# A windowed attention stage with sinks: ScalarE's and VectorE's pieces of a round in another order

## The reference, cut to what matters

```python
q = (x @ Wq.T + bq).reshape(B, S, 64, 64).transpose(0, 2, 1, 3)
k = (x @ Wk.T + bk).reshape(B, S, 8, 64).transpose(0, 2, 1, 3)    # each serves 8 query heads
v = (x @ Wv.T + bv).reshape(B, S, 8, 64).transpose(0, 2, 1, 3)
scores = jnp.einsum('bhqd,bhkd->bhqk', q, k) * scale
allowed = (qi >= kj) & (qi - kj < WINDOW)
scores = jnp.where(allowed[None, None], scores, -1e30)
logits = jnp.concatenate([scores, sink], axis=-1)
probs = jax.nn.softmax(logits, axis=-1)[..., :-1]
o = jnp.einsum('bhqk,bhkd->bhqd', probs, v)
return o.transpose(0, 2, 1, 3).reshape(B, S, H * HD) @ Wo.T + bo
```

## Time and profile before

| | us |
|---|---|
| median of 3 runs | 3887.63 (3885.69 to 3892.8) |
| the profiled execution | 3892.8 |
| its span in the profile | 3891.0 |
| PE busy | 3547.9 (91%) |
| DVE busy | 3078.6 (79%) |
| ACT busy | 2233.3 (57%) |
| POOL busy | 1442.3 (37%) |

### The profile page before, as it was taken

How to read it: one execution, slowest core, us unless ns; L and a number is a source line. 1 busy time by engine, 2 the same in 40 slices (tenths; PEclk the granted TensorE clock), 3 DMA queues, 4 the chain that set the end, 5 groups by cost and what they waited for, 6 DMA issues and landing times.

```text
span 3891.0 us, 93870 instructions
## 1 busy us (share of the span) xinstructions
PE 3547.9 (91%) x32894; PEld 2474.4 (64%) x32894; DVE 3078.6 (79%) x11272; ACT 2233.3 (57%) x6991; POOL 1442.3 (37%) x1741
## 2 busy tenths in 40 slices
PE   7999999999999989999989969989878999899955
PEld 5888888888888866666644433335556666555532
DVE  6989999999999966677779967767876778788771
ACT  5888888888888852257654433433333222467611
POOL 2455455455445510045448855520010000222117
PEclk8999999999999989889999989999988999799958
DMA  3000000000000012210000000000000000000023
GB/s 129 3 3 3 3 3 3 3 3 3 3 3 3 3 44 92 72 66 2 2 1 1 0 11 0 1 1 1 1 1 34 1 1 1 33 2 2 23 60 49
DMA packets 30897, 64.58 MB, mean 17 GB/s; under 512 B 3424, under 2 KB 19808, under 8 KB 29152
## 3 DMA queue, kind: packets, MB, share of 16 engines
q1 hardware_dynamic: 24288, 52.29, 3.8%
q0 software_dynamic: 6144, 6.30, 1.0%
HBM read 49.93 MB, written 8.65 MB: 15 GB/s over the span
## 4 chain that ended last, share of the span: by engine, by line
PE 67%; DVE 19%; issue 5%; ACT 5%; POOL 2%; DMA 1%; DVEq 0%; POOLq 0%; ACTq 0%; SPq 0%
PE ps L176 8%; PE ps L537 7%; PE ps L497 7%; PE ps L521 6%; PE ps L473 5%; PE ps L1674 3%; PE ps L1645 3%; PE ps L1643 3%; PE ps L2285 3%; PE ps L2298 3%; DVE gbbc L2337 2%; PE ps L1014 2%; DVE gbbc L2326 2%; DVE gbbc L2332 2%; PE ps L992 2%
## 5 line engine op out<-in xcount | busy, mean ns | idle before, releaser
L736 ACT ACTIVATE T<-T 128x128 f32<-128x128 f32 x1024 | 397.0, 398 | 11.6 <-DVE T L663 11.6
L736 ACT ACTIVATE W<-T 128x128 f32<-128x128 f32 x1024 | 396.9, 398 | 3.7 <-DVE T L663 3.7
L643 DVE CUSTOM_DVE_ANT_0 T<-ps,C 128x128 f32<-128x128 f32 x1536 | 381.3, 286 | 0.0
L653 DVE COPY_PREDICATED W<-gbbc,ps 128x512 f32<-128x512 int32 x512 | 342.5, 722 | 3.0 <-PE ps L176 2.5
L497 PE MATMUL ps<-T 64*64 64x192 f32 (+2 forms) x8192 | 317.8, 292 | 16.9 <-DVE T L643 16.9
L537 PE MATMUL ps<-W,gbbc 64*64 64x128 f32 (+1 forms) x6912 | 319.7, 310 | 2.0 <-DVE W L653 1.2
L497 PEld LDWEIGHTS ps<-T 64*64 64x64 f32 x8192 | 256.4, 133 | 95.8 <-issue 60.9
L176 PE MATMUL ps<-C,T 128*128 128x128 f32 (+1 forms) x1620 | 263.9, 301 | 50.4 <-DVE T L307 18.9
L1241 POOL TENSOR_TENSOR QK<-T,QK 128x512 fp32r<-128x512 f32 x128 | 162.0, 1275 | 383.3 <-ACT T L1201 264.9
L537 PEld LDWEIGHTS ps<-W,gbbc 64*64 64x64 f32 x6912 | 280.0, 132 | 28.2 <-PE ps L537 23.0
L827 POOL TENSOR_TENSOR W<-W,T 128x512 f32<-128x512 f32 x256 | 260.8, 1040 | 77.5 <-DVE T L670 77.5
(11 more groups left out here) (420 smaller groups left out, 8826.8 us busy)
## 6 DMA issues: line engine op xcount, KB each, us to landing
T<-crow_dram SPq DMA_DIRECT2D x128, 128.0 KB, 3.0
W<-in_l1f_dram SPq DMA_DIRECT2D x1, 6152.0 KB, 18.0
W<-in_l0a_dram SPq DMA_DIRECT2D x1, 5172.5 KB, 25.4
W<-in_l2f_dram SPq DMA_DIRECT2D x1, 3160.0 KB, 10.6
W<-in_l3f_dram SPq DMA_DIRECT2D x1, 3076.0 KB, 9.9
W<-in_sm_dram SPq DMA_DIRECT2D x1, 2729.0 KB, 9.0
W<-in_l0f_dram SPq DMA_DIRECT2D x1, 2256.0 KB, 30.2
X<-in_x_dram SPq DMA_DIRECT2D x1, 2048.0 KB, 7.4
```

Source lines behind the costliest of these rows:

```text
L643: done(e.tensor_tensor_reduce(sm[:, at:at + 128], src, m, 1.0, -3.0e38, ALU.add, ALU.max, mx[:, col:col + 1]), s["masked"], x == (3 if ban ...
L653: e.copy_predicated(a.PT[t % 2][:, 512 + 512 * j:1024 + 512 * j].rearrange("p (h w) -> p h w", h=4), is_.unsqueeze(1).broadcast_to([P, 4, ...
L736: done(e.activation(a.Pr[i % 4][:, at:at + w_], a.Sm[i % 2][:, at:at + w_], ACT.Exp, bias=a.ngs[i % 4][:, c:c + 1], scale=a.scale, accum_o ...
```

## The change

Two loops are written in another order. No instruction is added, taken away or altered.

On ACT, a full round's pieces between `outputs(2 * leaving)` and `sinks(2 * n)` are ordered anew: three of the weights of unit 2n come before the second `outputs`, three behind it, then `turned(2 * turning)`, and only then `project(ahead)`; the last two weights follow. On DVE, `parted(2 * turning)` and `shift(2 * n + 1)` change places.

```diff
@@ attention_dve
         if n is not None:
             masks(2 * n + 1)
+        if turning is not None:
+            parted(2 * turning)
         if n is not None:
             shift(2 * n + 1)
-        if turning is not None:
-            parted(2 * turning)
         if kv is not None:
             project(*kv)
@@ attention_act
         if leaving is not None:
             outputs(2 * leaving)
+        if n is not None:
+            begin(2 * n)
+            weights(2 * n, 0, 3)
+        if leaving is not None:
             outputs(2 * leaving + 1)
         if n is not None:
-            begin(2 * n)
-            weights(2 * n, 0, 4)
+            weights(2 * n, 3, 6)
+        if turning is not None:
+            turned(2 * turning)
         if ahead is not None:
             project(ahead)
-        if turning is not None:
-            turned(2 * turning)
         if n is not None:
-            weights(2 * n, 4, 8)
+            weights(2 * n, 6, 8)
             sinks(2 * n)
             begin(2 * n + 1)
             weights(2 * n + 1, 0, 2)
```

## The result

The changed kernel takes 3936.54 us (median of 4 runs, 3925.64 to 3940.66) against 3887.89 before (4 runs, 3885.69 to 3892.8). The ratio is 1.0119 with a 95% interval of 1.0097 to 1.0142, so it is slower by 38 to 55 us. The forecast was 3935.3, in a range of 3902 to 3958. The profiled execution took 3932.3, with a span of 3930.5.

The account below looks back on a forecast made before the run. PE was taken to bound the 10.28 us round; 110 rounds x 0.42 plus 15 x 0.10 = 47.7 us lost, giving 3940.5 from the profiled execution and 3935.3 us from the median of 3887.63, range 3902 to 3958.

Parts of the forecast that it names:

- What bounds the round: In the stage from 65 to 1382 us, PE's own instructions alone set the round of 10.28 us.
- the rival in which the change does not reach PE: The wait that holds the kv projection is for something other than L729; time stays at 3888 us, chance 0.03.
- The shift of L729: On ACT, the copy of q0 ends 4.61 us after the first L749, 0.95 us later than before.
- What PE makes of it: PE's transposes (L176) start 0.60 us after L729's end, so PE loses 0.42 us in each of 110 rounds.
- The early round: Round near 65 us where PE already waits for L729; its transposes start 0.60 us after the copy's end.
- the rival of 3904: L468's weight load goes ahead of the wait, so only its matmul is late, by 0.15 us a round; chance 0.04.
- Nothing is given back: PE's loss stays in the closed round, 10.70 us; rival with it given back loses 0.09 a round, 3898 us, chance 0.03.
- The 15 rounds behind a sequence's end: Rounds where DVE is late and PE waits 0.86 us at the second scores: a loss of only 0.10 us each.
- The second L749: On ACT, it releases PE's L521 load 0.04 us before PE gets there; costed at nothing.
- DVE's swap: L653 begins 0.09 to 0.11 us earlier and L663 1.34 later; cost 0, bounds -0.1 to +0.1 us a round.
- the rival that had it fall: New PE stops bring the granted clock to its lower level in one of eight rounds: 147 us more, 4082, chance 0.03.
- The faster rival: PE's 0.86 us waits for DVE's row maxima after every sequence go: 12.9 us less, 3875, chance 0.03.

Follow-up runs that it names:

- e1: Kernel before with only DVE's swap, parted ahead of shift: 3893.02 us against 3893.86, ratio 0.9991.
- e3: Changed kernel with project(ahead) (L729) put back ahead of turned(2 * turning) (L743): 3892.42 us against 3893.86 for the kernel before, ratio 1.0004.
- e4: Changed kernel with the key or value projection in another bank than q0's, so waiting for L743 instead of L729: 3888.65 us against 3893.86 before, ratio 0.9986.
- e5: Kernel before with only the second L749 moved behind three of the four weights: 3892.72 us in one run.
- e6: Kernel before with only L743 moved ahead of the pair L729: 3881.96 us in one run.
- e7: Changed kernel with all eight weights of a unit ahead of L729 instead of six: 4036.75 us in one run.
- e9: Kernel before with the second L749 behind all four weights, L729 in its old place: 3916.65 us in one run.
- e10: Changed kernel with four weights instead of three ahead of the second L749 and two behind it: 3936.22 us in one run.
- e8: Kernel before with DVE's two statistics of a finished sequence put one each into the next two rounds: 3874.26 us against 3888.97, ratio 0.9963.

## Why the prediction was right

*What bounds the round.* PE alone, as the forecast read it: nothing that left PE's releases in time changed the distance by more than 0.5 us (e1, e3, e4, e5, e6). That the loss is the wait for L729 is borne out by e3 and e4, which take it away in two ways, and by e7, which makes it larger; so the rival in which the change does not reach PE falls too.

*The shift of L729.* Forecast 4.61 us after the first L749, measured 4.57; the pair L729 takes 0.82 in the place of 0.84, the rest is hundredths in the L736 and in L743.

*What PE makes of it.* The early round gave 0.60 from L729's end to the transposes; measured 0.61. So a round lost 0.38 to 0.39 instead of 0.42. This is the term of the sum that was too large: 110 x 0.035 is 4 us, and 47.7 forecast against 43.6 in the stage is that difference. Most of it is L729's end, 0.04 us earlier than forecast. That the weight load does not go ahead of its wait is borne out (idle 0.52 on the load, 0.06 after the copy), and with it the rival of 3904 falls.

*Nothing is given back.* The idle of 0.33 ahead of the first scores, which might have been a hidden wait, is still 0.33:

```profile
608.25 0.53 PEld L497 LDWEIGHTS ps<-T 64*64 64x64 f32 x20 [0.33 <-issue]
```

*The 15 rounds behind a sequence's end.* Forecast 0.10. There ACT's first L736 waits for DVE, and the second scores start 0.86 late as before. From those scores to the transposes it was 5.13 us and is 682.10 - 676.89 = 5.21, so 0.08:

```profile
676.89 1.24 PE L497 MATMUL ps<-T 64*64 64x64 f32 x32 [0.86 <-DVE T L643]
...
682.10 1.04 PE L176 MATMUL ps<-C,W 128*128 128x128 f32 x8
```

*The second L749* had 0.04 us to spare by the forecast. It stayed clear of L521 in the changed kernel, and e9 and e10 show both halves of the argument: one weight more stops PE (e9), and that stop is hidden in the one at L468 (e10).

*DVE's swap.* Its size was misread: L653 starts 3.28 us after the round's first L749 before and 3.09 in e1, so 0.19 earlier and not 0.09 to 0.11. It has no share in the time (1247.2 against 1246.9).

*The clock* did not fall in the stage (1.00), so the rival that had it fall goes; stops of 0.5 us in every round do not lower it here, and neither do those of 1.3 us in e7, whose stage has 1.00 too. *The faster rival* needed the waits after a sequence to go. They did not with this change (12.0 us, 14 times), but e8 shows that they are worth what it said (13.5 us, forecast 12.9).

*The time.* The profiled execution was forecast at 3940.5 and took 3932.3: 4 us of the difference are the term above. The other 4 lie behind the last L705, where 2490.0 us (3930.5 - 1440.5) stand against 2494.1 before (3891.0 - 1396.9). The median's 48.65 holds the 43.6 of the stage; the remaining 5 is within the interval of the ratio, and no edit explains it. So it is partly luck that the forecast of 3935.3 lies only 1.2 us from the measured 3936.54: the stage's term was 4 us too large, and the medians differ by 5 us more than the stage does.

## What to carry to other kernels

Ask of each moved instruction not only who reads its result but who waits for the buffer that it empties, and compare two times: when the release comes in the new order (a sum of start distances in that queue) and when the waiting engine gets there. Up to the edge a delay is free (here 0.44 us of it, e3), just past it a part counts (0.38 of the next 0.47), and further on it counts in full (0.78 for 0.77, e7), in every round. Two late releases need not add up: when the second one's time is fixed by its own queue, as L729's is in e10, a stop at the first only shortens the stop at the second.

## What the runs showed that I had not expected

A stop of PE's weight loads costs less than their idle time: at L521 an idle of 0.34 us lengthens the round by 0.2 (e9), at L468 an idle of 0.52 by 0.38. The loads behind the stop run closer together, by 0.11 in both places: the eight of L521 take 1.59 in place of 1.70, the four of L468 0.52 in place of 0.63. Why is not shown.

The same kernel varied more between executions than its stage did: before, in 25 runs on one chip, from 3879.69 to 3916.18 us, while the 120 rounds between the first and the last L705 took 1246.9 to 1247.4 us in the kernel before and in all five versions whose edit cost nothing (e1, e3 to e6). What varies is the start (the first L705 at 145.9 to 150.1 in those six) and what lies behind the last L705 (2487.2 to 2496.2 us), both with a granted clock below 1.00 (0.82 in the first 65 us and 0.91 behind the stage, in the kernel before). In those 25 runs the fastest has a mean clock of 0.946 and the slowest 0.935; no run shows what makes it differ. For a change in one stage a distance between two landmarks of the profile told 1 us where medians told 8.

The wait of PE's score loads for PE's own scores (PEld L497 for PE L497) was 8.0 us between 100 and 1300 us before and 19.2 with DVE's swap (e1), at an unchanged distance. It does not follow the swap: e9 has 19.2 without it, and e7 has 8.0 with it. What sets it stays open; in e1 it costs nothing.
